# A routed expert loop that runs two blocks a turn, with three blocks outside it

## The reference

```python
scores = softmax(xt @ gate_w.T)                     # xt: 512 tokens x 512 features
_, idx = top_k(scores + gate_bias, 2)               # two of 8 experts for each token
for e in range(8):
    gate_e = sum(where(idx == e, weights, 0), axis=1)
    y = y + gate_e[:, None] * ((silu(xt @ w1[e].T) * (xt @ w3[e].T)) @ w2[e].T)
z = silu(xt @ sw1.T) * (xt @ sw3.T) @ sw2.T         # shared experts, every token
out = x + y + z
```

## Time and profile before

| | |
|---|---|
| median of 3 runs | 518.63 us (516.26 to 518.69) |
| the profiled execution | 517.0 us, of which 515.2 us is the span of its instructions |
| PE busy | 447.8 us, 87% |
| DVE busy | 325.2 us, 63% |
| granted clock of PE, mean | 0.927 of full speed |
| routed stage, first transpose of its rows to the last matmul | 376.8 to 493.2 us |
| routed blocks run | 12 |

### The profile page before, as it was taken

How to read it: one execution, slowest core, us unless ns; L and a number is a source line. 1 busy time by engine, 2 the same in 40 slices (tenths; PEclk the granted TensorE clock), 3 DMA queues, 4 the chain that set the end, 5 groups by cost and what they waited for, 6 DMA issues and landing times.

```text
span 515.2 us, 8206 instructions
## 1 busy us (share of the span) xinstructions
PE 447.8 (87%) x3200; PEld 310.2 (60%) x3200; DVE 325.2 (63%) x597; ACT 168.7 (33%) x209; POOL 68.0 (13%) x71
## 2 busy tenths in 40 slices
PE   1997997999968979899999599999988999999920
PEld 1962333455553566678884588884456888888710
DVE  5442236357964999996658956214139999999604
ACT  1102111227620011122232230121047878888400
POOL 1000000000003760004632100600000000000033
PEclk9999999899968878999969679999999999999985
DMA  8999809432041423028000200860069999999036
GB/s 324 430 426 427 357 0 407 165 97 67 1 164 32 133 50 118 3 69 343 1 1 3 81 0 1 293 239 1 0 254 377 397 382 408 389 408 374 30 97 188
DMA packets 18068, 97.04 MB, mean 188 GB/s; under 512 B 2817, under 2 KB 4481, under 8 KB 10497
## 3 DMA queue, kind: packets, MB, share of 16 engines
q1 hardware_dynamic: 14880, 81.88, 41.3%
q10 hardware_dynamic: 1872, 10.49, 5.8%
q0 software_dynamic: 1280, 4.20, 2.5%
HBM read 86.07 MB, written 13.63 MB: 194 GB/s over the span
## 4 chain that ended last, share of the span: by engine, by line
PE 75%; DVE 17%; issue 3%; DMA 2%; POOL 1%; ACT 1%; POOLq 0%; SPq 0%; ACTq 0%; DVEq 0%
PE bank L788 33%; PE bank L628 8%; PE bank L569 5%; PE bank L596 5%; PE bank L473 3%; PE bank L503 3%; PE bank L524 3%; DVE part L1273 3%; PE bank L483 3%; DVE ring L1273 3%; PE bank L612 1%; PE bank L758 1%; PE bank L776 1%; PE bank L459 1%; DVE x L1439 1%
## 5 line engine op out<-in xcount | busy, mean ns | idle before, releaser
L569 PE MATMUL bank<-xnT,ring 128*128 128x512 f32 x96 | 45.0, 622 | 0.7 <-ACT xnT L911 0.7
L1273 DVE SCALAR_TENSOR_TENSOR part<-ring,cols,part 128x504 f32<-128x504 f32 (+13 forms) x64 | 43.9, 747 | 0.1
L628 PEld LDWEIGHTS bank<-ring 64*64 64x64 f32 x960 | 36.1, 148 | 9.9 <-issue 9.0
L628 PE MATMUL bank<-ring 64*64 64x64 f32 (+1 forms) x960 | 40.4, 241 | 1.7 <-issue 1.6
L1273 DVE SCALAR_TENSOR_TENSOR ring<-bank,cols,ring 128x504 f32<-128x504 f32 (+2 forms) x36 | 26.4, 734 | 16.6 <-ACT ring L957 15.7
L596 PE MATMUL bank<-early,ring 128*32 128x512 f32 (+15 forms) x512 | 34.3, 414 | 0.0
L401 POOL TENSOR_TENSOR small<-small 128x1 f32<-128x1 f32 (+1 forms) x13 | 12.1, 928 | 161.9 <-DVE small L1160 95.4
L569 PEld LDWEIGHTS bank<-xnT,ring 128*128 128x128 f32 x96 | 18.5, 199 | 22.0 <-issue 20.9
L459 PE MATMUL bank<-consts,part 128*128 128x128 f32 x48 | 11.5, 396 | 21.0 <-DVE part L1166 14.1
L1055 ACT ACTIVATE rows<-bank 128x512 f32<-128x512 f32 x20 | 12.0, 598 | 46.1 <-PE bank L788 46.1
L1018 ACT ACTIVATE ring<-bank 128x256 f32<-128x256 f32 x20 | 7.7, 384 | 49.4 <-PE bank L628 48.9
(11 more groups left out here) (216 smaller groups left out, 941.4 us busy)
## 6 DMA issues: line engine op xcount, KB each, us to landing
early<-wffn_in SPq DMA_DIRECT2D x21, 1024.0 KB, 8.4
ring<-ctxT_in SPq DMA_DIRECT2D x4, 2048.0 KB, 27.4
ring<-ctx_in SPq DMA_DIRECT2D x4, 2048.0 KB, 31.8
raw1b<-wffn_in SPq DMA_DIRECT2D x7, 1024.0 KB, 10.6
raw3b<-wffn_in SPq DMA_DIRECT2D x7, 1024.0 KB, 7.5
raw2b<-wffn_in SPq DMA_DIRECT2D x7, 1024.0 KB, 9.0
ring<-firw_in SPq DMA_DIRECT2D x4, 1024.0 KB, 5.8
ring<-wqkv_in SPq DMA_DIRECT2D x1, 3072.0 KB, 12.8
```

Of the source, the lines that this page charges most:

```text
L569: last = pe.matmul(bank[5 + g % 3][:, :], wqkv[:, j, c, h * P:(h + 1) * P], xnT[:, c, :], start=(c == 0), stop=(c == DC - 1))
L628: last = pe.matmul(dst[s, d], left[s, L * t:L * (t + 1)], right(s, t), start=True, stop=True)
L1273: return dve.scalar_tensor_tensor(out=d, in0=s, scalar=w, in1=d, op0=ALU.mult, op1=ALU.add)
```

## The change

A turn of the loop holds two blocks, and three blocks stand outside it: 0 and 1 ahead, one behind. `last_group` is the block behind the loop less 2, `FIRST` (6) plus 2 for each of the numbers 9, 11 and 13 that is below the count of blocks needed. The blocks run are last_group + 3: 9, 11, 13 or 15, in place of 8, 12 or 16. `MAXB` is 15, so the zero fills are of 15 and 9 blocks. SBUF tensors lie at the same addresses.

```diff
-GB = 4
+GB = 2
 MINB = NTOK * TOPK // P
-MAXB = -(-(MINB + NE - 1) // GB) * GB
+MAXB = MINB + NE - 1
+PEEL = GB + 1
+FIRST = MINB + 1 - PEEL
...
-            return eng.value_load(expert_i[0:1, MAXB + GB - 1:], min_val=MINB - GB, max_val=MAXB - GB)
+            return eng.value_load(expert_i[0:1, MAXB + GB - 1:], min_val=FIRST, max_val=MAXB - PEEL)
...
             with sp.Fori(0, last_group, GB) as done:
-                for r in (-1, 0, 1, 2):
+                for r in (1, 2):
                     load_up(done + GB + r, r)
                     load_down(done + GB + r - 1, r - 1)
-            load_up(last_group + GB - 1, -1)
-            load_down(last_group + GB - 2, -2)
-            load_down(last_group + GB - 1, -1)
+            load_down(last_group + GB, 0)
...
             for p in range(2):
-                pool.wait_ge(st_y[p], last_group * 8 + 8 * GB)
+                pool.wait_ge(st_y[p], last_group * 8 + 16 * (GB - p))
...
             with pe.Fori(0, last_group, GB) as done:
                 J = done + GB
-                for r in (-2, -1, 0, 1):
+                for r in (0, 1):
                     step(J + r, r)
-            step(last_group + GB - 2, -2)
-            step(last_group + GB - 1, -1, more=False)
-            turn(last_group + GB - 1, -1)
-            routed_down(last_group + GB - 1, -1)
+            step(last_group + GB, 0, more=False)
+            turn(last_group + GB, 0)
+            routed_down(last_group + GB, 0)
...
-            firsts = nums.rearrange("p (g b) -> p g b", b=GB)[:, :, 0]
-            groups = owner[:, 0, 0:MAXB // GB]
+            firsts = nums[:, FIRST + PEEL:MAXB:GB]
+            more = (MAXB - FIRST - PEEL) // GB
+            groups = owner[:, 0, 0:more]
...
-            do(dve.tensor_scalar(expert[:, MAXB:], expert4[:, 0:1].broadcast_to([P, GB]), float(GB), -float(GB),
+            do(dve.tensor_scalar(expert[:, MAXB:], expert4[:, 0:1].broadcast_to([P, GB]), float(GB), float(FIRST),
                                  ALU.mult, ALU.add))
```

More of the change, by code:

```diff
@@ L1129, in _ @@
                 J = done + GB
-                for r in (-2, -1, 0, 1):
+                for r in (0, 1):
                     step(J + r, r)
[L1132 to L1135, removed]
+            step(last_group + GB, 0, more=False)
+            turned(last_group + GB, 0)
+            for r in (-1, 0):
                 keep_output(last_group + GB + r, r)
@@ L1533, in _ @@
             do(dve.tensor_scalar(expert[:, 0:MAXB], expert[:, 0:MAXB], float(NE - 1), None, ALU.min))
-            firsts = nums.rearrange("p (g b) -> p g b", b=GB)[:, :, 0]
-            groups = owner[:, 0, 0:MAXB // GB]
-            do(dve.tensor_tensor(groups, end[:, NE - 1:NE].broadcast_to([P, MAXB // GB]), firsts, ALU.is_gt))
+            firsts = nums[:, FIRST + PEEL:MAXB:GB]
+            more = (MAXB - FIRST - PEEL) // GB
+            groups = owner[:, 0, 0:more]
+            do(dve.tensor_tensor(groups, end[:, NE - 1:NE].broadcast_to([P, more]), firsts, ALU.is_gt))
             do(dve.tensor_reduce(expert4[:, 0:1], groups, AX, ALU.add))
-            do(dve.tensor_scalar(expert[:, MAXB:], expert4[:, 0:1].broadcast_to([P, GB]), float(GB), -float(GB),
+            do(dve.tensor_scalar(expert[:, MAXB:], expert4[:, 0:1].broadcast_to([P, GB]), float(GB), float(FIRST),
                                  ALU.mult, ALU.add))
@@ L1589, in _ @@
                 J = done + GB
-                for r in (-2, -1, 0, 1):
+                for r in (0, 1):
                     step(J + r, r)
-            step(last_group + GB - 2, -2)
-            step(last_group + GB - 1, -1, more=False)
-            turned(last_group + GB - 1, -1)
+            step(last_group + GB, 0, more=False)
+            turned(last_group + GB, 0)
             dve.wait_ge(S["x3_done"], NT)
```

## The result

The changed kernel took 510.61 us, the median of four runs from 508.37 to 511.63, against 518.66 us before (four runs, 516.26 to 523.48). The ratio is 0.9849, with a 95% interval from 0.9802 to 0.9895: faster by some 8 us, and the forecast was 509.0 in a range from 506.6 to 510.9. The profiled execution was 508.37 us with a span of 506.5 us, where the text forecast 507.9 and 506.1.

The account below looks back on a forecast made before the run. PE was taken to bound the routed stage, with DVE and DMA nearly full. -9.12 + 0.01 + 0.02 = -9.1 us gave 507.9 us from the profiled 517.0; 509.0 was taken from 507.2 to 509.6, range 506.6 to 510.9.

Parts of the forecast that it names:

- The step that leaves: Routed stage: one block fewer takes one full step out of PE's stream, -9.12 us.
- The count: Blocks needed are 11 by the reference's router, so 11 run; rival of another count 0.02, with 12 needed 526.1 us profiled.
- The branches: Loop: two more taken branches on each of four engines, covered; 0.01 us in all, at most 0.8 us.
- the lead of PE's sequencer: At the loop's branch PE's sequencer runs 2.3 us ahead of the array, so the branch's 0.4 us is covered.
- SP's turn: SP's branch issues raw1b's load 0.45 us later, hidden by 1.8 us of slack; nothing taken, 1.35 us if all passed on.
- The rival of late weights: Weight loads in the loop pass their slack, 0.45 us for each of three branches, 1.35 us; 510.4 by the median; chance 0.04.
- The fetch: Rival: each taken branch fetches its target behind weight traffic, 5.3 us a turn, 15.9 us, 523.8 us profiled; chance 0.02.
- The zero fills: Four blocks less of zeros, 2 MB less to move; no engine waits for it, so nothing.
- The end: POOL's wait at the end takes two store semaphores instead of one value: one more semaphore instruction, 0.02 us.
- The time: Whole kernel: 509.0 us by the median, 507.9 us profiled, range 506.6 to 510.9; the forecast's chance 0.92.

Follow-up runs that it names:

- the second profile: Profile of a rerun of the changed kernel, unchanged; stretch from block 2's first product to the last matmul 86.62 us, median of its six runs 509.69 us.
- The doses: Changed kernel with two, five or ten unused reads of an expert's number heading each turn on PE's sequencer; two: stretch 86.53 us; ten: ratio 1.0375, 540.23 us.
- 6 us later: Changed kernel with ten unused reads of an expert's number at the head of each turn on SP, ahead of raw1b's load; median 512.49 us.
- after_again: The changed kernel once more, unchanged, for the spread of its own profile; median 509.69 us of six runs, ratio 0.9832 to before.
- turns2_12: Kernel before with its eight loop blocks two to a turn, four turns in place of two, still 12 blocks; ratio 0.9998 to before.

## Why the prediction was right

- **The step that leaves.** -9.12 us forecast for the stage. Between before and after, the stretch that holds the loop fell by 95.77 - 86.72 = 9.05 us, with the second profile 9.15. Right, and by the reason given: PE's stream is full there, and runs with 9, 11, 12 and 13 blocks lie on one line.
- **The count.** 11 by the router's counts, and 11 loads and stores in the trace.
- **The branches.** 0.01 us forecast, at most 0.8. Two more of them alone: 0.03 us. The reason given was the lead of PE's sequencer, 2.3 us. The doses put it at 2.1 to 2.2 us: two reads hidden, five with 1.1 us of 3.3 showing, ten with 4.9 of 7.0. That was the claim with the least behind it, one branch in one profile, and it held.
- **SP's turn.** Forecast 0.45 us later and hidden. It is 0.27 us later (1.5 us between the two loads for 1.23 without a branch), and 6 us later are hidden too. The step was right; its slack was sized too small for the issue. I set 1.8 us, from the longest landing time, as if that time went with the load wherever it is put; 6.0 us of delay took 0.6 us of the slack at ACT. The rival of late weights, 510.4 us, went by the same error: at thirteen times its delay nothing comes late.
- **The fetch.** No turn shows it. The branch itself takes 0.21 to 0.25 us where it is taken, on PE, and is covered. A body of four blocks a turn, one of two and none at all agree within 0.4 us. In the changed kernel the queues of instruction loads moved a single packet (0.02 MB) from 396 to 484 us, with three taken branches on each of four engines, so no fetch went with each turn. The Trainium skill's rule (Runtime: NRT & Kernel Launch, Instruction fetch mechanics) that was weighed speaks of a target outside the window; no run here shows a stall at such a target.
- **The zero fills.** Nothing was forecast, and PE's stage began 0.3 us earlier, which is not resolved from one profile. The amount was counted double: four blocks of 256 KB are 1 MB less to write, not 2.
- **The end.** 0.02 us forecast for POOL's second wait. The tail grew by 0.66 us in this profile, but lies at 22.26 in the next one of the same kernel: it is not resolved below half a microsecond.
- **The time.** Forecast 509.0, measured 510.61 in four runs and 509.69 in six others. The sum was right to 0.1 us in the stage; what is left is the spread of the runs, of which I knew four within 2.4 us of each other. It is wider: single runs of the kernel before lie between 513.96 and 524.28 us, and the forecast's range held the median with 0.3 us to spare. The mechanism was right, but that a range of 4.3 us held a median of four runs was partly luck, when six runs of the same kernel lie 9.9 us apart.

No version ran that beats the changed kernel by more than the runs differ. The one without a loop is 0.3 us shorter in its stretch and right for one count alone.

## What to carry to other kernels

Where one engine is full for all of a padded block, a coarser rounding costs that engine's whole step for each padded block, and the trip count of the loop can be made finer at no price that these runs resolve (0.1 us), as long as what a turn adds to the engine's sequencer is shorter than the time by which that sequencer is ahead of its array. A load's time from issue to landing under a full stream is no measure of how early it has to be issued: move its issue and look, or look at what lies ahead of it in the queue. When a kernel's runs differ by more than a change is worth, cut the profile at points that the change doesn't touch, and compare the pieces.

## What was not expected

The runs of one kernel differ by 10 us, and the granted clock of PE goes with it. Over the six runs of `after_again` the mean clock falls as the time grows, from 0.930 at 505.45 us to 0.905 at 515.34 us, and the profiles show it in single stretches. Those of `turns2_12` and `after_again` do the same work up to the routed stage, but for the zero fills and small tables, and reach it at 382.82 and at 375.76 us. The shared experts' first products, 12 matmuls of 128x512 each, first with the longer span, then with the shorter (start us, us):

```profile
300.33 5.47 PE L788 MATMUL bank<-xe,w1a 128*128 128x512 f32 x12
305.60 3.27 PE L788 MATMUL bank<-xe,w3a 128*128 128x512 f32 x12
...
317.78 5.47 PE L788 MATMUL bank<-xe,w1a 128*128 128x512 f32 x12
323.04 3.06 PE L788 MATMUL bank<-xe,w3a 128*128 128x512 f32 x12
```

```profile
297.54 4.73 PE L788 MATMUL bank<-xe,w1a 128*128 128x512 f32 x12
302.11 2.89 PE L788 MATMUL bank<-xe,w3a 128*128 128x512 f32 x12
...
313.33 2.99 PE L788 MATMUL bank<-xe,w1a 128*128 128x512 f32 x12
316.16 2.88 PE L788 MATMUL bank<-xe,w3a 128*128 128x512 f32 x12
```

The granted clock of the product in the third row is at its lower level in the one run and full in the other (columns as in the earlier trace rows):

```profile
317.78:323.04 5.26, 5.26 (x13) 4.11 (x14) 4.67 (x19) 0.00 (x0) 0.00 (x0) 0.50 0.00 0
```

```profile
313.33:316.16 2.83, 2.83 (x14) 2.34 (x14) 2.76 (x5) 0.00 (x0) 0.00 (x0) 1.00 0.00 0
```

These are the same instructions, 5.47 us in the one run and 2.99 in the other, behind the same small matmuls of 128x8, in which PE was not idle. The routed stage's first product does it again. PE is idle for 0.87 us, does four transposes and is idle for 1.46 us ahead of it in every profile, and then it takes about 4.5 us in eight of the twelve and about 3.0 us in four. Here it is 4.54 us in one, at a granted clock of 0.62 from 384.91 to 389.29 us, and 3.01 in the other, at 1.00.

```profile
384.91 4.54 PE L788 MATMUL bank<-w1a,xgT 128*128 128x512 f32 x12 [1.46 <-issue]
```

```profile
377.85 3.01 PE L788 MATMUL bank<-w1a,xgT 128*128 128x512 f32 x12 [1.46 <-issue]
```

The one run is 2.8 us behind the other at the first of these rows and 7.1 us at the routed stage. So the clock was at its lower level behind the same work or the same pause in one run and not in another, and that alone is 2.5 us at the one place and 1.5 us at the other, which comes on top of the 7.1. Where the first 2.8 us come from was not followed up. What decides between the levels stays open too: no experiment here was made on it.
